# Narrower routed rows and a closing sum on chip in a two-layer attention and mixture-of-experts kernel on one Trainium2 core

## The reference, cut to what matters

```
h = layernorm(x) * (1 + ca) + sa ;  x = x + ga * attention(h)
h = layernorm(x) * (1 + cb) + sb ;  x = x + gb * ffn(h)          # gb: one row of 256 per batch
# ffn of layer 1:
t = h * rsqrt(mean(h*h) + eps) * norm_w
G[m, e] = softmax over the 4 best logits of t @ gate_w.T + gate_b   (else 0)
y_e = (min(a, 7) * sigmoid(1.702 a) * (clip(b, -7, 7) + 1)) @ w2_e + b2_e,   a, b = t @ w1_e + b1_e
ffn(h) = h + sum_e G[m, e] * y_e
```

## Time and profile before

| | |
|---|---|
| time, median of 3 runs | 1031.97 us (1031.87 to 1034.49) |
| the profiled execution | 1035.23 us, of it the span of the trace 1033.1 us |
| PE busy | 966.9 us (94%) |
| DVE, ACT, POOL busy | 725.7, 673.3 and 426.7 us |
| moved by DMA | 180.53 MB |
| last matrix product ends | 1003.1 us into the span |

### The profile page before, as it was taken

How to read it: one execution, slowest core, us unless ns; L and a number is a source line. 1 busy time by engine, 2 the same in 40 slices (tenths; PEclk the granted TensorE clock), 3 DMA queues, 4 the chain that set the end, 5 groups by cost and what they waited for, 6 DMA issues and landing times.

```text
span 1033.1 us, 20537 instructions
## 1 busy us (share of the span) xinstructions
PE 966.9 (94%) x6036; PEld 818.0 (79%) x6036; DVE 725.7 (70%) x2546; ACT 673.3 (65%) x1944; POOL 426.7 (41%) x447
## 2 busy tenths in 40 slices
PE   8999999999999999999999999996879889999980
PEld 5769878878988887887888788885767679999970
DVE  3564656787767687777669677865888678888870
ACT  2757767668677767768767875783746457777740
POOL 3322411421461362255146136323166646565662
PEclk9999999999999999999999999998999899999995
DMA  9927991993799420020012004237258788999954
GB/s 307 305 87 243 376 375 69 355 378 131 287 363 378 174 79 1 22 94 22 1 67 70 2 12 165 64 131 281 61 164 184 208 238 219 222 223 223 217 111 81
DMA packets 93677, 180.53 MB, mean 175 GB/s; under 512 B 9901, under 2 KB 29037, under 8 KB 92669
## 3 DMA queue, kind: packets, MB, share of 16 engines
q1 hardware_dynamic: 73467, 148.55, 43.2%
q0 software_dynamic: 18752, 30.30, 13.1%
q10 hardware_dynamic: 1346, 0.36, 0.2%
HBM read 77.71 MB, written 107.99 MB: 180 GB/s over the span
## 4 chain that ended last, share of the span: by engine, by line
PE 81%; DVE 7%; issue 4%; DMA 3%; ACT 1%; POOL 1%; another core or an unknown queue 1%; ACTq 1%; SPq 0%; DVEq 0%; POOLq 0%
PE bank L1112 12%; PE bank L1076 10%; PE bank L1048 10%; PE bank L1121 5%; PE bank L1066 5%; PE bank L1038 5%; PE bank L1027 4%; PE bank L998 3%; PE bank L1067 3%; PE bank L1057 2%; PE bank L1037 2%; PE bank L913 2%; PE bank L904 2%; PE bank L982 2%; PE bank L1020 2%
## 5 line engine op out<-in xcount | busy, mean ns | idle before, releaser
L1908 POOL TENSOR_TENSOR RB<-RB 128x512 f32<-128x512 f32 x64 | 66.7, 1042 | 277.1 <-DVE RB L1687 276.7
L1112 PE MATMUL bank<-RB 128*128 128x128 f32 x1264 | 157.3, 278 | 5.3 <-DVE BC L1801 2.3
L1112 PEld LDWEIGHTS bank<-RB 128*128 128x128 f32 x1264 | 150.4, 194 | 8.3 <-DVE BC L1801 3.4
L1377 ACT ACTIVATE RB<-RA,nw 128x512 f32 x158 | 105.4, 715 | 48.9 <-issue 22.3
L1076 PE MATMUL bank<-RA,RB 128*128 128x256 f32 x512 | 132.5, 381 | 1.1 <-ACT RB L1278 1.1
L1048 PE MATMUL bank<-RA 128*128 128x256 f32 x512 | 121.4, 380 | 0.3 <-DMA RA<-in_L_attn_Wq 0.3
L1048 PEld LDWEIGHTS bank<-RA 128*128 128x128 f32 x512 | 94.6, 190 | 15.6 <-issue 2.8
L1076 PEld LDWEIGHTS bank<-RA,RB 128*128 128x128 f32 x512 | 91.3, 190 | 14.4 <-issue 2.3
L1884 POOL TENSOR_TENSOR qs<-qs,half 128x4 f32<-128x4 f32 x64 | 65.6, 1024 | 63.8 <-DVE qs L1696 56.1
L1121 PE MATMUL bank<-RB,BC 128*128 128x256 f32 x316 | 83.1, 387 | 8.3 <-DVE BC L1814 7.3
L1278 ACT ACTIVATE RB<-bank 128x256 f32<-128x256 f32 x128 | 48.7, 381 | 45.8 <-PE bank L1067 43.9
(11 more groups left out here) (254 smaller groups left out, 2416.3 us busy)
## 6 DMA issues: line engine op xcount, KB each, us to landing
xsD<-BC SPq DMA_DIRECT2D x17, 4232.0 KB, 32.8
RB<-in_w2b SPq DMA_DIRECT2D x79, 256.0 KB
RB<-xsD SPq DMA_DIRECT2D x61, 264.5 KB
BC<-modD SPq DMA_DIRECT2D x16, 512.0 KB, 4.1
X<-xsD SPq DMA_DIRECT2D x18, 264.5 KB, 3.2
RA<-in_w SPq DMA_DIRECT2D x2, 2048.0 KB, 7.2
RA<-in_w SPq DMA_DIRECT2D x6, 512.0 KB, 8.6
RA<-in_L_attn_Wq SPq DMA_DIRECT2D x1, 2048.0 KB, 13.9
```

The lines of the kernel that those rows point to most:

```text
L1112: m = pe.matmul(ps[:, 128 * j:128 * j + 128], WS[:, n % 2, c, 128 * j:128 * j + 128], XT[:, n % 2, c * 128:c * 128 + 128], start=(c == 0), ...
L1377: m = act.activation(WS[:, n % 2, c, :], W1[:, bass.ds(r, 1), c, :].rearrange("p a n -> p (a n)"), ACT.Copy, scale=nw[:, c:c + 1])
L1908: pool.tensor_tensor(sq, qrow, qrow, ALU.mult).then_inc(mine("q_sq", p), 1)
```

## The change

Routed rows are 273 floats wide instead of 529. `f_gb` goes, and with it what waited for it (`f_send`, two `bc`). `y_out` becomes a `tensor_scalar` of the product, the gate weight and 0.5. `store` and `merge` go, with their waits in `xb`, in `y_add` and at SP's end. Both accumulators, `accA` and `accB`, begin at zero: `acc_zero` issues two DMAs of 2 MB. The rings of row blocks lie elsewhere: of the first five places one in SC, one in RC and three in a slot of BC, so that blocks 1 and 2 to 4 wait for the last `q_t` and for `s_x(6, 1)`. At the end, when the last two `y_add` have landed, SP reads `accA` and ACT reads `accB` back into SBUF, batch by batch (8 DMAs of 256 KB each); a `join` per batch adds the two, multiplies by `gb` (`gains`, loaded during the blocks) and adds X, on DVE for six batches and on POOL for batches 2 and 5; and SP writes each batch to `out` (`put`).

```diff
-NBLK, REG, ROW = 79, 2048 + 128, 529
+NBLK, REG, ROW = 79, 2048 + 128, 273
+JOIN_POOL = 2, 5
-                on.wait_ge(*done("store", (PART if n < FIRST else NB) - 1))
-                pool.indirect_dma_start((out_r, accD)[n % 2], ...
+                pool.indirect_dma_start((accA, accB)[n % 2], ...
-                dve.scalar_tensor_tensor(YB[n % 5], psum("y_out", n)[:, 0:256], rows(n)[:, bass.ds(ex[n] + 257, 1)], rows(n)[:, 273:529], ALU.mult, ALU.mult)
+                dve.tensor_scalar(YB[n % 5], psum("y_out", n)[:, 0:256], rows(n)[:, bass.ds(ex[n] + 257, 1)], 0.5, ALU.mult, ALU.mult)
-                    if n == RINGS[0] - 1:
+                    if n == 1:
                         on.wait_ge(*done("q_t", NU // 2 - 1))
                         on.wait_ge(*done("q_sq", NU // 2 - 1))
+                    elif 1 < n < RINGS[0]:
+                        on.wait_ge(*done("s_x", NB - 2, 1))
-                sp.dma_start(accD.rearrange("(a p) n -> p a n", p=128), zz...)
+                for acc in (accA, accB):
+                    sp.dma_start(acc.rearrange("(a p) n -> p a n", p=128), zz...)
-            def merge():
-                on.wait_ge(*done("y_add", NBLK - 2))
-                on.wait_ge(*done("y_add", NBLK - 1))
-                pool.dma_start(out_r..., accD..., accum_op=ALU.add, max_dma_last_dim=8192)
+            def sum_a(b):                                   # SP; sum_b(b) is the same on ACT
+                on.wait_ge(*done("w_in", NBLK - 1))
+                on.wait_ge(*done("y_add", NBLK - 1 - NBLK % 2))
+                on.wait_ge(*done("y_add", NBLK - 2 + NBLK % 2))
+                sp.dma_start(sumA[:, 2 * b:2 * b + 2, :], acc_v[0][:, 2 * b:2 * b + 2, :])
+            def join(b):                                    # DVE, and POOL for b in JOIN_POOL
+                dve.tensor_tensor(t, t, sumB[:, 2 * b:2 * b + 2, :], ALU.add)
+                dve.tensor_tensor(t, t, gains[:, b:b + 1, :].broadcast_to([128, 2, 256]), ALU.mult)
+                dve.tensor_tensor(t, t, x, ALU.add)
+            def put(b):                                     # SP
+                on.wait_ge(*done("join", b))
+                sp.dma_start(out_v[:, b, :, :], sumA[:, 2 * b:2 * b + 2, :])
```

More of the change, by code:

```diff
@@ L62 @@
 }
-HOP, LANDING = 0.2, {"bc": 5.0, "mod_store": 4.0, "clear": 14.0, "w12": 11.0, "xb": 3.2, "w2x": 3.5, "y_add": 4.0, "f_send": 3.0, "store": 4.0}
+HOP, LANDING = 0.2, {"bc": 5.0, "mod_store": 4.0, "clear": 14.0, "w12": 11.0, "xb": 3.2, "w2x": 3.5, "y_add": 4.0, "f_send": 3.0}
 LANDED = {"x0": 4.5, "cT": 4.0, "wmA": 6.0, "wk": 10.0, "wv": 11.5, "wq": 17.0, "wo": 24.0, "x": 30.0, "wmB": 45.0, "wm1": 50.0, "sw": 55.0, "small1": 55.0, "tables": 20.0, "w0": 60.0}
@@ L403, in ffn1 @@
             for k in range(4):
-                yield do("f_send", 1, b, i, k, slot=b % 4, by=16, aside=(b > 3), after=[("f_gb", b), ("clear", 2 * b + 1)])
+                yield do("f_send", 1, b, i, k, slot=b % 4, by=16, aside=(b > 3), after=[("clear", 2 * b + 1)])
     def offsets(b):
@@ L413, in offsets @@
         if b + 2 < NB:
-            yield do("bc", 1, b + 2, slot=4 + b % 2, by=16, aside=True, after=[("f_gb", b)])
+            yield do("bc", 1, b + 2, slot=4 + b % 2, by=16, aside=True)
         yield do("f_x", b)
-        yield do("store", b, by=16)
     def spread(part):
@@ L432, in block @@
     def block(n):
-        after = [("n_bi", 0), ("store", PART - 1), ("f_send", 1, PART - 1, 1, 3)] + [("q_t", NU // 2 - 1)] * (n == RINGS[0] - 1) + [("y_out", n - RINGS[0]), ("tok", n - RINGS[0])] * (n >= RINGS[0])
+        after = [("n_bi", 0), ("f_send", 1, PART - 1, 1, 3)] + [("q_t", NU // 2 - 1)] * (n == 1) + [("s_x", NB - 2, 1)] * (1 < n < RINGS[0]) + [("y_out", n - RINGS[0]), ("tok", n - RINGS[0])] * (n >= RINGS[0])
         yield do("xb", n, slot=n % RINGS[0], by=16, after=after)
@@ L525, in lay_out @@
             load_block(n + ahead)
-    p.add("merge", by=16)
+        if n == lo + 16:
+            p.add("gains", by=16)
+    for b in range(NB):
+        p.add("sum_a", b, slot=b, by=16)
+        p.add("sum_b", b, slot=b, by=16)
+    for b in range(NB):
+        p.add("join", b, slot=b in JOIN_POOL)
+        p.add("put", b, by=16)
     return p
@@ L541, in build @@
         macc_set = ctx.enter_context(nc.semaphore("macc_set"))
-        own = {e: ctx.enter_context(nc.semaphore(f"{e}_own")) for e in ("dve", "act")}
+        own = {e: ctx.enter_context(nc.semaphore(f"{e}_own")) for e in ("dve", "act", "pool")}
         def done(stage, *key):
@@ L555, in build @@
         xsD = nc.dram_tensor("xsD", (128 + 16 * REG, ROW), F32, kind="Internal").ap()
-        accD = nc.dram_tensor("accD", (2048, 256), F32, kind="Internal").ap()
+        accA, accB = (nc.dram_tensor(f"acc{i}", (2048, 256), F32, kind="Internal").ap() for i in "AB")
         RA = sb("RA", [128, 16384])
@@ L733, in build @@
         out_v = out.rearrange("b (t p) d -> p b t d", p=128)
-        out_r = out.rearrange("b s d -> (b s) d")
+        acc_v = [acc.rearrange("(j p) n -> p j n", p=128) for acc in (accA, accB)]
         block = ctx.enter_context(nc.Block())
@@ L865, in _ @@
                     run[stage](*key)
-            on.wait_ge(*done("store", NB - 1))
-            on.wait_ge(*done("merge"))
+            on.wait_ge(*done("put", NB - 1))
         @block.tensor
@@ L1300, in f_src @@
                 m.then_inc(mine("f_src", b), 1)
[L1302 to L1307, removed]
             def f_ht(l, b):
@@ L1384, in x_out, with sum_b @@
                 act.activation(XT[:, n % 2, :], psum("x_out", n)[:, 0:256], ACT.Copy).then_inc(mine("x_out", n), 1)
+            def sum_b(b):
+                on.wait_ge(*done("w_in", NBLK - 1))
+                for n in (NBLK - 2, NBLK - 1):
+                    on.wait_ge(*done("y_add", n))
+                act.dma_start(sumB[:, 2 * b:2 * b + 2, :], acc_v[1][:, 2 * b:2 * b + 2, :]).then_inc(mine("sum_b", b), 16)
             def e_tanh(n):
@@ L1821, in y_out @@
                     on.wait_ge(*done("y_add", n - 5))
-                dve.scalar_tensor_tensor(YB[n % 5], psum("y_out", n)[:, 0:256], rows(n)[:, bass.ds(ex[n] + 257, 1)], rows(n)[:, 273:529], ALU.mult, ALU.mult).then_inc(mine("y_out", n), 1)
+                dve.tensor_scalar(YB[n % 5], psum("y_out", n)[:, 0:256], rows(n)[:, bass.ds(ex[n] + 257, 1)], 0.5, ALU.mult, ALU.mult).then_inc(mine("y_out", n), 1)
             def ones_v():
@@ L1877, in _ @@
         def _(pool):
-            on = Once(pool)
+            on, own_ = Once(pool), Chain(own["pool"])
             pool.dma_start(cb16[:, :], I["cb16"]).then_inc(L["cb16"], 16)
```

70 lines of the change are left out of this document (45 added, 25 removed), and 4 rows, old and new, of the table ENGINE.

## The result

The changed kernel takes 1052.38 us (median of 4 runs, 1050.31 to 1053.89) against 1033.23 us of the kernel before on the same chip: 1.0178 times as long, interval [1.0156, 1.0200]. That is slower by some 18 us, and above the range that was forecast. The profiled execution took 1051.81 us, its span 1049.7 us.

What follows compares the result with a forecast made beforehand. PE was taken as the bound until the attention ends and in the blocks, with gaps from 760 to 850 us and 30 us without PE last. -5.2, -3.3 and +10.5 make +2.0 on 1031.97: 1034.0 us, range 1026.5 to 1040.5.

Steps and rivals of the forecast that it cites:

- part 2: PE's stretch with gaps, 760 to 850 us: shorter landing, no f_gb or store, fewer stalls, -3.3 us; bounds -8 and +4.
- part 3: Second zero fill, new wait for s_x(6, 1), y_out as tensor_scalar and gains: said to move nothing.
- the gaps: PE's idle time of 6.2 and 8.8 us between 760 and 850 us; forecast gain 3.3 us.
- backlog: y_adds going out late behind their y_outs during the blocks; narrower rows were to remove this, -5.2 us.
- Bounds of the kernel now: PE never idle from 100 us until attention ends, gaps 760 to 850 us, full again in blocks, 30 us without PE.
- Part 1: Narrower rows in the blocks: DMA share to about 0.75, landing near 5 us, late y_adds gone, -5.2 us.
- Part 4: New end after the last y_add lands at T: loads, join with DVE and POOL blocking each other, put; T + 24.5, +10.5 us.
- the backlog stays: Rival: y_add still lands in 6 us whatever the load, so narrower rows gain nothing there; 1039.2 us, chance 0.2.
- the end is cheap: Rival: DVE and POOL don't block each other in join, transfers bound the end; +6.2 us, 1029.7 us, chance 0.2.
- The gaps go: Rival: landing times keep PE waiting from 760 to 850 us, halved rows save some 8 us; 1029.3 us, chance 0.2.
- The planner's order is worse: Rival: the planner's new order costs +4 us in place of -3.3; 1041 us, chance 0.05.

Runs made afterwards that it cites:

- loads_behind: Changed kernel with its stages in the order of the kernel before, and xb(2) to xb(4) moved behind the transfers of w12(2): 1039.49 us, 1.0045.
- new_order_before: Kernel before with all its work, its stages laid out in the order of the changed kernel: 1051.09 us, 1.0163.
- narrow_rows: Kernel before in its own order, with rows of 273, no f_gb, and y_out without the batch's gate factor: 1031.37 us, 0.9966.
- joins_on_dve: Changed kernel with all eight join on DVE and none on POOL: 1049.65 us, 1.0140.

## Why the prediction was wrong

The steps that failed are the -3.3 us of part 2 and the nothing of part 3. I counted the planner's new order as at most a gap or two, and it cost 10.2 us in the changed kernel and 16.8 in the kernel before; the gaps gained nothing; and the wait of three loads cost 3.5 us in the old order. The loss of 1.78%, 18.4 us, by ratios of the runs, taken away in this sequence:

| part | forecast | measured | from |
|---|---|---|---|
| the planner's order | in part 2, bound +4 | +10.2 (6.5 to 13.9) | 1.0178 - 1.0079 |
| the wait of the loads, in the old order | 0 (part 3) | +3.5 | 1.0079 - 1.0045 |
| gaps, narrower rows | -3.3 | 0 | windows of `loads_behind` |
| backlog | -5.2 | -3.5 | 1 - 0.9966 |
| the end | +10.5 | +8 | the rest; the traces give +7.5 |

Another sequence gives another split. With the order taken first, as `new_order_before` has it, it is 16.8 us, and 1.6 are left for backlog, end and loads, where the rows above have 8. So 10.2 and 16.8 are two readings of the order's share, and how it interacts with the rest is open; that the three loads went out at another time is one candidate (680 us in `new_order_before`, which has no such wait, and 699 in the changed kernel).

- **Bounds of the kernel now**: right for the kernel before, but I took "PE is never idle until the attention ends" for a property of the work. It was one of the order. It was also a little too strong: rows 1 show the stretch up to 200 us, and PE is idle for 3.9 us in all between 100 and 706 us.
- **Part 2 failed, and decided the case.** I named the new order, gave it a bound of +4 us ("a gap or two") and gave the rival a chance of 0.05; its price, 1041 us, even lay above my range. Nothing in the trace of before could bound it: the 6 us and 9 us of idleness there were the price of that order, not of its neighbours. The order could have been had without a chip, by laying out both plans and comparing them: 744 of 1265 positions differ. The size, as far as I can see, could not. The other half of the part failed too: halved rows gained nothing in the gaps, so neither the landing of 6.44 us nor `store` and `f_gb` were what PE waited for in the end.
- **Part 3**: the second zero fill, `y_out` and `gains` cost nothing that shows (the stretch 100 to 200 us is unchanged). The wait for `s_x(6, 1)` did cost 3.5 us in the old order. I asked what SP must issue next and not what else goes on while its three loads run.
- **Part 1**: the backlog went, as I had it; -3.5 and not -5.2. The landing near 5 us on which I put it is not shown, only that the `y_add`s keep the pace of 5.75 us. I had `y_add(75)` go out with its `y_out`; in `narrow_rows` it goes out 1.5 us later, and PE ends 0.8 us later. Traffic fell as reckoned: 181 GB/s in `narrow_rows` from 900 to 950 us is 0.81 of 223, and the changed kernel's 200 has the 1 MB of `gains` on top. The DMA share fell only to 0.84 and 0.86, not 0.75: the narrower rows took more of the engines' time per byte. From 100 to 200 us, where the table is cleared, it is 0.67 at 161 GB/s against 0.82 at 291.
- **Part 4**: direction and mechanism right. Blocking is shown: DVE's five operations beside POOL's took 4.9 us more than alone (I had given it 4.3, T + 24.5 against T + 20.2), and `joins_on_dve` takes it away with POOL's share of the work, net 2.9 us in the traces. The last `put` landed at T + 25.7 (forecast 24.5), since batch 3 landed at T + 10.2 and not at T + 8.2 and both engines' operations were stretched. Against that, the 4.5 us that I left standing behind the last transfer went: they belong to POOL. So the end is T + 26.1 and not T + 29, +7.5 us.
- The rule of the Trainium skill on shared interfaces ("GPSIMD Engine Reference", Key points) held. What I had not taken from it is the price for POOL: four of its own operations took 1.48 to 1.59 us beside DVE's, and not 1.09. Its first took 1.26 us beside an idle DVE, so that part of the difference is no contention.
- **Rivals**: "the backlog stays" and "the end is cheap" did not come. "The gaps go" fell by the windows of `loads_behind`. "The planner's order is worse" was the true one, at more than twice its price.

Open: what holds ACT at `o_out(126)`, what the late loads cost in the new order, and which of the waits in the new order carries its 10 to 17 us; I read PE's stalls (4.5 us of idleness between 690 and 712 us, and lower clock behind them), but did not take single ones away.

## What to carry to other kernels

Where a program lays out the order of the work, every edit of a stage, a weight or a wait is also an edit of the order of everything: lay out both and compare them before costing anything else, and try the new work in the old order first. Here two unlike neighbours of a favourable order were 12 to 17 us worse, where I had read 4 at most out of its trace; how often that is so elsewhere, two orders can't tell. A load that is "off the path" still has a moment at which it runs, and moving it is an edit to be costed.

## What the runs showed of the hardware

- A transfer issued last by POOL held the end of the program for 4.5 us behind its landing, with `merge` and with a plain 256 KB `put`; one issued by SP for 0.4 us.
- DVE and POOL with both operands in SBUF side by side: 128x512 additions and products took 1.63 to 1.75 us on DVE (alone 0.69), each ending 0.5 us behind POOL's, and 1.26 to 1.59 us on POOL (1.26 beside an idle DVE).
- Rows of 273 floats in place of 529 cut the bytes moved per second beside the blocks to 0.81 (223 to 181 GB/s) and the DMA engines' share only from 0.93 to 0.84.
